# Two routed feed-forward layers and two image gates on one core: POOL's turn rewritten, column sums by halves, a square root moved ahead

## The chip, the cores and the metric

One core of one Trainium2 chip runs the whole program. The metric is device time in microseconds (us) of one launch. The kernel before took 1337.18 us, the median of 3 runs (1332.98 to 1341.03).

## The reference

`x` is (16, 256, 16, 16) in float32. All four steps add to their input:

```python
x = x + conv0(ln_c(x))     # 32 groups of 8 channels, gated by rows and columns
t = tokens(x);  t = t + ffn0(ln_t(t))   # 4096 tokens of 256, 8 experts, top 2
x = x + conv1(ln_c(x))     # 1x1 convolution 256 -> 256 with bias
t = tokens(x);  t = t + ffn1(ln_t(t))   # 8 experts, top 2, hidden 1024, biases

def branch(ph, pw):        # conv0, once with means, once with maxima
    hw = conv1x1(concatenate([ph, pw], axis=2))
    ah, aw = hw[:, :, :h], hw[:, :, h:]
    return gnorm(g * sigmoid(ah)[..., None] * sigmoid(aw)[:, :, None, :])
x1 = branch(g.mean(axis=3), g.mean(axis=2))
y1 = branch(g.max(axis=3), g.max(axis=2))
weights = softmax(mean of x1) . y1 + softmax(max of y1) . x1
out = g * sigmoid(weights)
```

In `ffn0` an expert is `silu(x w1) * (x w3)` times `w2` with hidden 512; in `ffn1` it is `silu(x v1 + b1)` times `v2` plus `b2` with hidden 1024.

## The kernel before, in words

Five engines run one instruction stream each and meet at semaphores: PE (matmul), DVE (vector), ACT (scalar), POOL (GpSimd) and SP (DMA queue). Nothing is scheduled by a planner; the order on each engine is the order of the source.

**First convolution.** The normed image is turned so that channels lie on partitions: `g`, two blocks `k` of 4096 values (16 images of 16 x 16). For `r` = 0 (sums) and 1 (maxima) and both `k`, DVE reduces every image along its rows (L1065) and along its columns (L1066, a strided view), 16 lines of 16 values each, and PE and ACT turn the lines into gates (L600, L838). POOL multiplies three of the four blocks `(r, k)` by the row gates (L239) and then by the column gates (L244), the third after DVE has given the gates of `r` = 1 their sign (L1088); DVE does the fourth with the same two operations. Both engines' inputs lie in SBUF. DVE then takes statistics (L1078), maxima (L1081), and the deviation (function `deviations(4)`: seven small operations, a square root by ACT at L805, five more from L1018). Softmax, a table of mixing weights and the last stage follow: for each of 16 images DVE writes four 128 x 128 masks (L1143, function `masks`), PE mixes (L617), ACT takes the sigmoid (L849), DVE multiplies, PE turns back, DVE adds and takes statistics.

**Pieces.** Beside this ACT sums absolute values of 64 pieces of 256 KB of the second layer's weights (`sum_pieces`, L830). SP loads them into three buffers, each as soon as the piece three before is summed. Pieces 0 to 19 stand in ACT's order ahead of the gates of `r` = 1, pieces 20 to 63 behind them and ahead of the square root.

**Expert stages.** Each layer sorts its 8192 token copies into 35 tiles of 256 rows, grouped by expert. For tile `n`: POOL gathers the rows by an indirect DMA each for two halves (`fetch`, L458) into one of two buffers `x_rows`; SP turns them by DMA transposes into one of two buffers `x_cols` (`turn_rows`, L360); PE multiplies up (L712) and down (L734); ACT and DVE work between; the result goes into the single buffer `y_rows`, and POOL adds it into DRAM by two indirect DMAs (`put`, L498). POOL's loop is by turns, one tile each: `put(n)` waits for tile n-1's stores to land, copies two lists of row numbers, waits for `y_copied` and issues the stores; then `fetch_next(n + 2)` copies two lists again (L505) and issues the gathers of tile n + 2. Each wait on a count that is a register stands in a loop of one pass (`after`).

In the first layer ACT does per tile: four silus (L927), four copies (L931), the high halves of one piece of the second layer's weights (`split_hi`, L903), then `move_pieces` (L911: two waits; L895: a store of 512 KB; L285, L286: two loads of 256 KB for the next tile's `split_hi`), and last the copy of the result into `y_rows` (L946). DVE multiplies (L1403), takes low halves (L1407), waits for `y_free`, chooses the next tile's token weights (`pick_weights`, L1380, L1383) and computes the low halves of the piece (L1337). In the second layer PE has 96 matmuls a tile, DVE writes the result (L1418), and ACT scales it (L953).

## Time and profile before

| | before |
|---|---|
| median of 3 runs | 1337.18 us |
| the profiled execution's own time | 1330.54 us |
| its span, first to last instruction | 1328.7 us |
| mean granted TensorE clock | 0.830 |
| busy, share of the span: PE, DVE, ACT, POOL | 72%, 61%, 45%, 38% |
| first convolution | from about 0 to 208 us |
| experts of layer 0, from the first copy of a result to the last | 382 to 721 us |
| second convolution and routing | about 730 to 895 us |
| experts of layer 1 | 905 to 1296 us |

Busy shares are averages over stages whose limits differ. What the change is worth is read stage by stage, from the wait that ends last there. In the rows below a start and a duration in us stand first; in brackets stands the idle time of the engine just before, and what ended it.

### The profile page before, as it was taken

What the parts mean: (1) busy time and instruction counts of PE and PEld (TensorE: products, weight loads), DVE (VectorE), ACT (ScalarE), POOL (GpSimd) and SP (SyncE); (2) the same over time, 40 slices, a digit from 0 to 9 for tenths busy, and PEclk for the clock granted to TensorE, in tenths of its full rate; (3) what the DMA queues carried; (4) which work ended last, traced back from release to release, by engine and by line L of the source; (5) the groups of instructions that cost most, each with busy time, mean ns of one, the idle gap of its engine ahead of it and who ended that gap; (6) DMA issues with size and microseconds to landing.
All of it is one profiled execution on the core that took longest, in us unless ns stands there. A gap on an engine that the chain in (4) does not pass through costs nothing.

```text
span 1328.7 us, 28374 instructions
## 1 busy us (share of the span) xinstructions
PE 954.9 (72%) x7185; PEld 790.8 (60%) x7185; DVE 806.6 (61%) x1970; ACT 595.0 (45%) x1332; POOL 509.3 (38%) x479
## 2 busy tenths in 40 slices
PE   5210375637688888888885388457999899999984
PEld 4100264624667666676774277426888787888873
DVE  6999488779755455455553676683455455555550
ACT  5265422228655555555553023283444344444442
POOL 1285000000036555666564140003555555556550
PEclk8655596555899999999998695558999999999996
DMA  7066204961857888888887704304555554554448
GB/s 254 1 198 209 75 0 118 337 186 48 269 125 183 182 180 174 186 194 192 192 182 182 257 0 153 109 1 95 120 104 117 127 122 85 135 134 75 77 74 264
DMA packets 210851, 189.97 MB, mean 143 GB/s; under 512 B 98992, under 2 KB 184440, under 8 KB 210680
## 3 DMA queue, kind: packets, MB, share of 16 engines
q1 hardware_dynamic: 150632, 108.48, 28.5%
q0 software_dynamic: 27440, 38.97, 18.3%
q10 hardware_dynamic: 32736, 42.02, 9.8%
q8 instruction: 18, 0.29, 0.1%
q14 instruction: 25, 0.20, 0.1%
HBM read 111.22 MB, written 58.79 MB: 128 GB/s over the span
## 4 chain that ended last, share of the span: by engine, by line
PE 34%; DMA 22%; issue 17%; DVE 11%; ACT 6%; ACTq 3%; POOL 2%; DVEq 1%; SPq 1%; POOLq 1%
PE bank L734 12%; PE bank L712 12%; DMA wreg<-in_L_ffn_w_dram 7%; DMA region<-rows_x,fetch_now 5%; DMA rows_y<-region,put_now 5%; PE bank L645 4%; DMA xt<-region 3%; PE bank L562 2%; PE bank L617 1%; POOL rows_y L498 1%; ACT wreg L830 1%; PE bank L770 1%; DVE region L1066 1%; PE bank L687 1%; DVE region L1418 1%
## 5 line engine op out<-in xcount | busy, mean ns | idle before, releaser
L712 PE MATMUL bank<-xt,wreg 128*128 x3360 | 391.0, 278 | 59.3 <-DMA xt<-region 52.1
L712 PEld LDWEIGHTS bank<-xt,wreg 128*128 128x128 f16 x3360 | 331.1, 100 | 113.5 <-issue 69.1
L498 POOL DMA_INDIRECT rows_y<-region,put_now x140 | 240.0, 1714 | 189.5 <-ACT region L953 87.7
L734 PE MATMUL bank<-wreg,region 128*128 128x256 f16 x2520 | 291.5, 274 | 24.0 <-DVE region L1413 13.9
L734 PEld LDWEIGHTS bank<-wreg,region 128*128 128x128 f16 x2520 | 242.4, 98 | 64.8 <-DVE region L1413 16.4
L458 POOL DMA_INDIRECT region<-rows_x,fetch_now x144 | 145.9, 1013 | 158.7 <-issue 82.6
L936 ACT ACTIVATE region<-bank,b_t,wreg 128x256 f32<-128x256 f32 x280 | 135.6, 562 | 20.6 <-issue 12.2
L953 ACT ACTIVATE region<-region 128x256 f32<-128x256 f32 x70 | 31.7, 500 | 207.3 <-DVE region L1418 202.0
L1410 DVE TENSOR_SCALAR region<-region,wreg 128x512 f16<-128x512 f32 x140 | 71.0, 507 | 65.6 <-ACT region L936 57.6
L1413 DVE SCALAR_TENSOR_TENSOR region<-region,wreg 128x512 f16<-128x512 f32 x140 | 105.2, 752 | 5.0
L562 PE MATMUL bank<-ident,xn 128*128 128x128 f32 x256 | 54.4, 372 | 58.9 <-DVE xn L1037 52.8
L1418 DVE SCALAR_TENSOR_TENSOR region<-bank,wreg,region 128x512 f32<-128x512 f32 x35 | 26.3, 751 | 109.8 <-PE bank L734 76.6
L1403 DVE SCALAR_TENSOR_TENSOR region<-bank,fac,region 128x256 f32<-128x256 f32 x140 | 64.1, 480 | 41.0 <-ACT region L927 33.6
L562 PEld LDWEIGHTS bank<-ident,xn 128*128 128x128 f32 x256 | 44.3, 202 | 66.8 <-DVE xn L1037 58.7
L927 ACT ACTIVATE region<-bank,fac 128x256 f32<-128x256 f32 x140 | 62.5, 470 | 37.2 <-PE bank L712 33.8
L645 PE MATMUL bank<-gate_w,xt 128*128 128x8 f32 x256 | 57.1, 361 | 18.8 <-DVE st_lg L1183 18.8
L645 PEld LDWEIGHTS bank<-gate_w,xt 128*128 128x128 f32 x256 | 55.8, 330 | 24.6 <-issue 24.1
L946 ACT ACTIVATE region<-bank,region 128x256 f32<-128x256 f32 x70 | 29.4, 471 | 86.1 <-issue 58.9
L1380 DVE TENSOR_TENSOR region<-region (+1 forms) x72 | 11.8, 163 | 92.5 <-DMA rows_y<-region,put_now 76.9
L1337 DVE SCALAR_TENSOR_TENSOR wreg<-wreg x70 | 49.5, 749 | 29.2 <-issue 24.6
L931 ACT ACTIVATE region<-region 128x256 f16<-128x256 f32 x140 | 57.1, 415 | 21.8 <-DVE region L1403 16.5
L458 POOL DMA_INDIRECT region<-rows_x,first_rows x4 | 4.4, 1099 | 155.0 <-DVE first_rows L1312 154.4
(241 smaller groups left out, 1312.5 us busy)
## 6 DMA issues: line engine op xcount, KB each, us to landing
wreg<-in_L_ffn_w_dram SPq DMA_DIRECT2D x48, 512.0 KB, 6.8
wreg<-in_L_ffn_w_dram ACTq DMA_DIRECT2D x72, 256.0 KB
split_v<-wreg ACTq DMA_DIRECT2D x36, 512.0 KB
wreg<-in_L_ffn_w_dram SPq DMA_DIRECT2D x64, 256.0 KB, 3.0
wreg<-split_v SPq DMA_DIRECT2D x32, 512.0 KB
rows_x<-region SPq DMA_DIRECT2D x16, 512.0 KB, 4.5
rows_y<-tok SPq DMA_DIRECT2D x16, 512.0 KB, 4.9
tok<-rows_y SPq DMA_DIRECT2D x16, 512.0 KB, 6.0
```

The lines of the kernel that those rows point to most:

```text
L458: nc.gpsimd.indirect_dma_start(x_bits[:, b, r, 0:C + 2], None, rows_x[f], bass.IndirectOffsetOnAxis(ap=row_list, axis=0)).then_inc(xr_load ...
L498: nc.gpsimd.indirect_dma_start(rows_y[f], bass.IndirectOffsetOnAxis(ap=put_now[:, g_:g_ + 1], axis=0), y_rows[:, g_, :], None, compute_op= ...
L562: last = pe.transpose(to[:, k, h * P:(h + 1) * P], xn[:, j, h, k * P:(k + 1) * P], ident[:])
L645: last = pe.matmul(zb[j][:, h * E:(h + 1) * E], xt[:, j, k, h * P:(h + 1) * P], gate_w[:, f, k], start=(k == 0), stop=(k == KC - 1))
L712: last = pe.matmul(to, block, x_cols[:, bass.ds(b, 1), :, xs_, k, :].rearrange("p j r n -> p (j r) n"), start=(k == 0 and ws_ + xs_ == 0), ...
L734: last = pe.matmul(yb[:, r * C:(r + 1) * C], lhs[:, c, r * P:(r + 1) * P], block, start=first, stop=end, skip_group_check=True)
L927: act.activation(gate_act[:, h, (c % 2) * TILE:(c % 2 + 1) * TILE], zb[c][:, 0:TILE], ACT.Silu, scale=fac[f][:, 0, e:e + 1]).then_inc(silu ...
L931: act.activation(hid_hi[:, c], hid[:, h, (c % 2) * TILE:(c % 2 + 1) * TILE], ACT.Copy).then_inc(hi_ready[f], 1)
L936: last = act.activation(gate_act[:, h, c * TILE:(c + 1) * TILE], zb[h][:, c * TILE:(c + 1) * TILE], ACT.Silu, bias=b1_t[:, e, 2 * h + c:2 ...
L1403: dve.scalar_tensor_tensor(half(hid[:, h], c), zb[c][:, TILE:2 * TILE], fac[f][:, 1, e:e + 1], half(gate_act[:, h], c), ALU.mult, ALU.mult ...
L1410: dve.tensor_scalar(to_hi, gate_act[:, h], fac[f][:, 1, e:e + 1], None, ALU.mult).then_inc(hi_ready[f], 1)
L1413: dve.scalar_tensor_tensor(to_lo, gate_act[:, h], fac[f][:, 1, e:e + 1], to_hi, ALU.mult, ALU.subtract).then_inc(lo_ready[f], 1)
```

## The change

1. **POOL's turn.** Three tiles are gathered ahead of the loop instead of two having been fetched and a third begun. A turn `t` copies all four lists at once into one of two buffers (`copy_lists`), gathers tile t + 3, and then stores tile t. The gathers wait for the transposes of tile t + 1 and for its token weights. DVE therefore picks the weights of tile n + 1 at the top of tile n's body, into four slots rather than two. In layer 0 DVE no longer waits for `y_free`.
2. **ACT in layer 0.** `move_pieces` stands behind the copy of the result.
3. **Column lines.** The strided reduction becomes four tensor_tensor operations: the 16 x 16 image is added (or compared) by halves, 2048, 1024, 512 and 256 values wide.
4. **Square root ahead of sums.** ACT takes the square root after 46 pieces, four more follow, and the other 14 stand by twos behind the sigmoids of the mixing loop, which is unrolled on ACT.
5. **Masks.** Four operations become one tensor_tensor with two broadcast inputs.

```diff
-                for r in range(2):
-                    fetch(f, 0, r, first_rows[:, r:r + 1])
+                def first_fetch(n):
+                    for r in range(2):
+                        free(pool, xr_loaded[r][f], 16 * n)
+                        free(pool, xc_ready[r][f], 16 * (n - 1))
+                        free(pool, weights_ready[f], n - 1)
+                        fetch(f, n % 2, r, first_rows[:, 2 * n + r:2 * n + r + 1])
+                first_fetch(0)
                 total = pool.value_load(bounds[0:1, E:E + 1], min_val=E, max_val=TILES)
+                first_fetch(1)
...
-                def put(n, copied):
-                    pool.wait_ge(y_free[f], 32 * n + 16)
-                    nc.gpsimd.tensor_copy(put_now[:], moves[:, bass.ds(2 * n, 2), 1]).then_inc(puts_copied[f], 1)
-                    after(n, lambda m: pool.wait_ge(puts_copied[f], m + 1))
-                    after(copied, lambda m: pool.wait_ge(y_copied[f], m))
...
                 with pool.Fori(0, total // 2) as p:
                     for b in range(2):
-                        put(2 * p + b, 2 * p + b + 1)
-                        fetch_next(2 * p + b + 2, 1 - b)
+                        t = 2 * p + b
+                        for r in range(2):
+                            pool.wait_ge(xr_loaded[r][f], 16 * t + 48)
+                        copy_lists(t, b)
+                        def may_fetch(m):
+                            pool.wait_ge(lists_copied[f], m + 1)
+                            for r in range(2):
+                                pool.wait_ge(xc_ready[r][f], 16 * m + 32)
+                            pool.wait_ge(weights_ready[f], m + 2)
+                        after(t, may_fetch)
+                        for r in range(2):
+                            fetch(f, 1 - b, r, now[:, b, r, 0:1])
+                        after(t, lambda m: pool.wait_ge(y_copied[f], m + 1))
+                        put(b)
...
-            sum_pieces(20, 2 * PIECES)
+            sum_pieces(20, 46)
             deviation(4)
+            sum_pieces(46, 50)
...
-            pairs(act, mix_gates)
+            for i in range(HB):
+                mix_gates(i)
+                sum_pieces(50 + 2 * i, min(52 + 2 * i, 2 * PIECES))
...
                             split_hi(n)
-                            move_pieces(n)
                             act.wait_ge(y_ready[f], n + 1)
...
                             last.then_inc(y_copied[f], 1)
+                            move_pieces(n)
...
-                    dve.tensor_reduce(line[:, r, k, :, HW:2 * HW], v.rearrange("p b h w -> p b w h"), AX.X, op).then_inc(lines_ready, 1)
+                    half, n = g[:, k, :].rearrange("p (b n) -> p b n", b=NB), L // 2
+                    free(dve, lines_ready, 2 * (r * KC + k))
+                    while n > HW:
+                        chain(dve.tensor_tensor(fold[:, :, 0:n], half[:, :, 0:n], half[:, :, n:2 * n], op))
+                        half, n = fold, n // 2
+                    dve.tensor_tensor(line[:, r, k, :, HW:2 * HW], half[:, :, 0:HW], half[:, :, HW:2 * HW], op).then_inc(lines_ready, 1)
...
-                for r in range(2):
-                    for k in range(KC):
-                        last = dve.tensor_scalar(mix[:, j, r, k], in_group[:], coef[:, r, k, bass.ds(2 * i + j, 1)],
-                                                 None, ALU.mult)
-                last.then_inc(mix_ready[j], 1)
+                dve.tensor_tensor(mix[:, j].rearrange("p r k n -> p (r k) n"), in_group[:].unsqueeze(1).to_broadcast([P, 2 * KC, P]),
+                                  coef[:, :, :, bass.ds(2 * i + j, 1)].rearrange("p r k b -> p (r k) b").to_broadcast([P, 2 * KC, P]),
+                                  ALU.mult).then_inc(mix_ready[j], 1)
...
                     with dve.Fori(edges[e], edges[e + 1]) as n:
+                        pick_weights(f, n + 1)
...
-                        else:
-                            dve.wait_ge(y_free[f], 32 * n + 16)
-                        pick_weights(f, n + 1)
```

DVE's stream in the first convolution, before, from the first lines to the signs (`wreg` is `g`, `region` holds the lines and the partial sums):

```order
L1057 TENSOR_TENSOR region<-region 128x128
L1065 TENSOR_REDUCE region<-wreg 128x16x16
L1066 TENSOR_REDUCE region<-wreg 128x16x16
L1065 TENSOR_REDUCE region<-wreg 128x16x16
L1066 TENSOR_REDUCE region<-wreg 128x16x16
```

The same two blocks after the change:

```order
L1076 TENSOR_TENSOR region<-region 128x128
L1084 TENSOR_REDUCE region<-wreg 128x16x16
L1088 TENSOR_TENSOR region<-wreg 128x2048
L1088 TENSOR_TENSOR region<-region 128x16x64
L1088 TENSOR_TENSOR region<-region 128x16x32
L1090 TENSOR_TENSOR region<-region 128x16x16
L1084 TENSOR_REDUCE region<-wreg 128x16x16
L1088 TENSOR_TENSOR region<-wreg 128x2048
L1088 TENSOR_TENSOR region<-region 128x16x64
L1088 TENSOR_TENSOR region<-region 128x16x32
L1090 TENSOR_TENSOR region<-region 128x16x16
```

Each column reduction, one operation with one input, became four operations with two inputs in SBUF. They stand in the stretch in which POOL's gates run.

ACT's stream in one tile of layer 0, before, from the second high half of the piece (L903) to the store of the last piece (L895), ahead of which stand the two waits of `move_pieces` (L911); the two loads and then the copy of the result follow:

```order
L903 ACTIVATE wreg<-wreg 128x512
L911 UNCONDITIONAL_BRANCH
L911 ISA x2
L911 COMPARE_AND_BRANCH
L911 UNCONDITIONAL_BRANCH
L911 ISA
L911 COMPARE_AND_BRANCH
L895 ISA x3
L895 DMA split_v<-wreg 128x2048
```

And after, from the same high half (L922) on; L964 is the copy of the result, and L930 begins the waits of `move_pieces`, behind which the store and the loads stand:

```order
L922 ACTIVATE wreg<-wreg 128x512
L960 REGISTER_ALU
L961 ISA
L964 ISA
L964 ACTIVATE region<-bank,region 128x256
L964 ISA
L964 ACTIVATE region<-bank,region 128x256
L930 UNCONDITIONAL_BRANCH
L930 ISA
```

The two ACTIVATEs of the result, and the waits they carry, now stand between the high halves of a piece and the loads of the next piece.

## Rows read from the trace of the kernel before

**Rows 1.** Timeline, first convolution, DVE and POOL: start, us, engine, line.

```profile
45.34 6.97 DVE L1066 TENSOR_REDUCE region<-wreg 128x256 f32<-128x4096 f32 x1
52.23 4.41 DVE L1065 TENSOR_REDUCE region<-wreg 128x256 f32<-128x4096 f32 x1
...
56.75 7.18 POOL L239 TENSOR_TENSOR wreg<-wreg,region 128x4096 f32<-128x4096 f32 x1 [52.24 <-ACT region L838]
...
64.01 8.87 POOL L244 TENSOR_TENSOR wreg<-wreg,region 128x4096 f32<-128x4096 f32 x1
...
80.10 8.88 POOL L244 TENSOR_TENSOR wreg<-wreg,region 128x4096 f32<-128x4096 f32 x1
...
86.56 2.43 DVE L1072 TENSOR_TENSOR region<-region 128x1 f32<-128x1 f32 x1
...
94.90 4.43 DVE L239 TENSOR_TENSOR wreg<-wreg,region 128x4096 f32<-128x4096 f32 x1
94.94 11.41 POOL L239 TENSOR_TENSOR wreg<-wreg,region 128x4096 f32<-128x4096 f32 x1 [5.97 <-DVE region L1088]
...
99.36 11.28 DVE L244 TENSOR_TENSOR wreg<-wreg,region 128x4096 f32<-128x4096 f32 x1
```

**Rows 2.** Timeline, pieces 20 and 63 on ACT, and DVE behind the square root.

```profile
91.59 0.62 ACT L830 ACTIVATE wreg<-wreg 128x512 f32<-128x512 f32 x1
...
145.06 0.63 ACT L830 ACTIVATE wreg<-wreg 128x512 f32<-128x512 f32 x1 [0.71 <-DMA wreg<-in_L_ffn_w_dram]
...
147.38 0.55 DVE L1018 RECIPROCAL xt<-xt 128x64 f32<-128x64 f32 x1 [10.52 <-ACT xt L805]
```

**Rows 3.** Timeline, mixing loop, DVE: a product of 512 values, then four masks.

```profile
161.83 0.69 DVE L1153 TENSOR_TENSOR region<-region,wreg 128x512 f32<-128x512 f32 x1 [4.09 <-ACT region L849]
162.44 0.87 DVE L1143 TENSOR_SCALAR region<-region 128x128 f32<-128x128 f32 x4
```

**Rows 4.** Timeline, experts of layer 0, ACT: the first and the last copy of a result.

```profile
382.11 0.84 ACT L946 ACTIVATE region<-bank,region 128x256 f32<-128x256 f32 x2 [2.38 <-DVE region L1393]
...
721.29 0.84 ACT L946 ACTIVATE region<-bank,region 128x256 f32<-128x256 f32 x2 [3.68 <-issue]
```

**Rows 5.** Timeline, experts of layer 0, ACT and its queue: from loads to next result.

```profile
410.45 0.40 ACTq L286 DMA_DIRECT2D wreg<-in_L_ffn_w_dram  x1
...
411.15 0.84 ACT L946 ACTIVATE region<-bank,region 128x256 f32<-128x256 f32 x2 [2.27 <-issue]
...
416.54 1.33 ACT L903 ACTIVATE wreg<-wreg  x2 [1.04 <-DMA wreg<-in_L_ffn_w_dram]
...
420.14 0.84 ACT L946 ACTIVATE region<-bank,region 128x256 f32<-128x256 f32 x2 [2.26 <-issue]
```

**Rows 6.** Timeline, experts of layer 0: one turn of POOL, and the landing of stores.

```profile
595.27 1.62 POOL L498 DMA_INDIRECT rows_y<-region,put_now  x1 [2.31 <-ACT region L946]
...
597.20 1.58 POOL L498 DMA_INDIRECT rows_y<-region,put_now  x1 [0.30 <-issue]
...
600.46 1.04 POOL L458 DMA_INDIRECT region<-rows_x,fetch_now  x1 [1.48 <-DMA xt<-region]
...
602.42 0.16 DVE L1380 TENSOR_TENSOR region<-region  x1 [3.52 <-DMA rows_y<-region,put_now]
602.56 0.84 ACT L946 ACTIVATE region<-bank,region 128x256 f32<-128x256 f32 x2 [2.35 <-DMA rows_y<-region,put_now]
...
604.33 1.62 POOL L498 DMA_INDIRECT rows_y<-region,put_now  x1 [1.35 <-ACT region L946]
```

**Rows 7.** Timeline, experts of layer 0, PE: the up part of three tiles.

```profile
400.29 5.43 PE L712 MATMUL bank<-xt,wreg 128*128 x48 [1.65 <-DMA xt<-region]
408.40 5.43 PE L712 MATMUL bank<-xt,wreg 128*128 x48
419.57 7.10 PE L712 MATMUL bank<-xt,wreg 128*128 x48 [2.90 <-DMA xt<-region]
```

**Rows 8.** Waits over the whole span: DVE's result of layer 1 behind stores.

```profile
DVE region L1418 <- DMA rows_y<-region,put_now: 33.2, 6, 7.2
```

More of the change, by code:

```diff
@@ L83, in bass_metaformer @@
         sig = region[:, 2048:4096].rearrange("p (r k b l) -> p r k b l", r=2, k=KC, b=NB)
+        fold = region[:, 4096:6144].rearrange("p (b n) -> p b n", b=NB)
         rows = region[:, :].bitcast(F16).rearrange("p (t c) -> p t c", t=NT)
@@ L259, in bass_metaformer @@
         listed, list_taken = sem("listed"), sem("list_taken")
-        fetches_copied, puts_copied = two("fetches_copied"), two("puts_copied")
+        lists_copied = two("lists_copied")
         ids_listed = sem("ids_listed")
@@ L526, in all_done, with may_put @@
+                        put(b)
+                last = total // 2 * 2
+                copy_lists(last, 0)
+                def may_put(m):
+                    pool.wait_ge(lists_copied[f], m + 1)
+                    pool.wait_ge(y_free[f], 32 * m + 16)
+                after(last, may_put)
+                after(total, lambda m: pool.wait_ge(y_copied[f], m))
+                put(0)
                 def all_done(m):
@@ L1377, in pick_weights @@
                     dve.wait_ge(xr_loaded[r][f], 16 * n + 16)
-                side = n if isinstance(n, int) else n % 2
-                one = lambda v: v[:, bass.ds(side, 1)]
-                dve.tensor_tensor(one(weighed), one(x_weights), choice[:, bass.ds(2 * n, 2), :].rearrange("p (j g) k -> p j g k", j=1),
+                one = lambda v, sides: v[:, bass.ds(n if isinstance(n, int) else n % sides, 1)]
+                dve.tensor_tensor(one(weighed, 2), one(x_weights, 2), choice[:, bass.ds(2 * n, 2), :].rearrange("p (j g) k -> p j g k", j=1),
                                   ALU.mult).then_inc(weighed_ready[f], 1)
                 dve.wait_ge(weighed_ready[f], n + 1)
-                dve.tensor_reduce(one(weights), one(weighed), AX.X, ALU.add).then_inc(weights_ready[f], 1)
+                dve.tensor_reduce(one(weights, 4), one(weighed, 2), AX.X, ALU.add).then_inc(weights_ready[f], 1)
             def experts(f, edges):
```

40 lines of the change are left out of this document (14 added, 26 removed).

## The prediction

> **What bounds the kernel now.** I read the busy time by stretches first, to see the stages, then the timeline of the three places that the diff touches, and the waits last. No engine is full over the whole span; each stage has its own limit.
>
> In the first convolution DVE is busy nearly without a gap, and POOL's gates run beside it. The thing to see there is how the two engines treat each other [rows 1]. POOL's row gates take 7.18 us alone and its column gates 8.87. The third time, started 0.04 us after DVE's own L239, the row gates take 11.41: 7.18 plus 4.23, which is DVE's whole operation. DVE's L244, issued at 99.36, takes 11.28 though it has the size of L239 (4.43): 6.85 more, about what POOL still had to do (94.94 + 11.41 = 106.35). And L1072, a product of one element per partition, takes 2.43 us: it ends at 88.99, when POOL's L244 ends (80.10 + 8.88 = 88.98). So a tensor_tensor on DVE with both inputs in SBUF and a running POOL gate exclude each other for a whole instruction, and at an end the one that has waited goes first. The reductions L1065 and L1066 (4.41 and 6.97 us) are not slowed beside POOL: with one input they pass.
>
> Behind that, DVE is ready for the square root at 147.38 - 10.52 = 136.86 and waits 10.52 us, since ACT first finishes all 64 pieces [rows 2].
>
> In the experts of layer 0 a tile takes (721.29 - 382.11) / 34 = 9.98 us [rows 4]. PE alone needs 8.11: where it had no wait, up part followed up part at that distance [rows 7]. PE waits for the transposes, hence for the gathers, which POOL issues behind the stores. POOL's turn has hardly a pause of its own choice: 595.27 to 604.33 is stores, copy, gathers, copy [rows 6]. Two other loops run close behind. The store loop: stores at 595.27, landed by 602.4, copy of the result at 602.56, next stores at 604.33, which makes 9.06 us [rows 6]. The loop of the pieces: loads issued by 410.85, landed by 416.54 (5.7 us; the idle time before L903 is laid to this DMA), then high halves, waits, a store, two loads and the result at 420.14 [rows 5]; this gives 420.14 - 411.15 = 8.99 us.
>
> In the experts of layer 1 PE is nearly full; stores held DVE up six times, for 33.2 us of DVE's time, of which PE lost only part [rows 8].
>
> **The change part by part.**
>
> Column lines. By 4.43 us for 4096 values and 0.69 for 512 [rows 1, 3] a value costs 1.04 ns and an operation 0.15 us. The four steps (2048, 1024, 512, 256 values) cost 2.29 + 1.22 + 0.69 + 0.42, and with the gaps between 4.75, against 6.97: 2.2 less per block, if they are let through. Now the order of events, by the rule read from rows 1:
> - Block (0,0) ends at 45.3 + 4.8 = 50.1. The next row reduction ends at 54.5. POOL's first gate followed these lines by 56.75 - 52.31 = 4.4, so it too wants to start at 54.5. Whoever is first, one half-sum (2.3), POOL's 7.2, POOL's 8.9 (which gets its turn at the first gap in DVE's chain) and the other half-sums (2.4) come one after another: the lines of (0,1) are ready at 75.3, not at 63.6.
> - POOL's second gates start some 3 us later (the 4.4 without the loading of ACT's table), at 78.4. DVE reduces rows until 79.7 and then waits until 85.6; a half-sum to 87.9, POOL to 96.8, the rest to 99.2.
> - Block (1,1) has no POOL beside it, which waits for the signs: 4.4 + 4.8, to 108.4. Before, the lines were done at 86.3. That is 22.1 later; L1072 no longer waits 2.3, so the signs and all behind them are 19.9 later (94.9 becomes 114.8), and DVE is ready for the square root at 156.8.
>
> The Trainium skill has this as a rule that speaks against the change: in "SBUF — State Buffer", section "Who interferes with whom", a DVE instruction with two SBUF inputs and a GpSimd instruction that reads SBUF hold the shared port in turn, each for its whole length, while a tensor_reduce on trn2 never contends. By that rule the stage ends 10 us later, without it 17 us earlier; the trace agrees with it, by the 2.43 us of L1072.
>
> Square root ahead. A piece takes (145.06 - 91.59) / 43 = 1.24 us [rows 2]. Pieces 20 to 45 begin behind the gates of r = 1, now at about 111.4, and end at 144, before 156.8. So the wait of 10.5 us is gone: L1018 comes at about 157.2 in place of 147.38, which is 9.8 later. The four pieces behind the root (three are loaded, the fourth's load can be issued only after the first) and the load of the table for the exponential push it back by 0 to 1 us more, I take 0.7. The 14 others fit into ACT's idle time in the mixing loop, where ACT works less than half of it; if they did not, each pair would cost up to 1.5 us for 7 rounds.
>
> Masks. One product of 512 values (0.69) for four masks (0.87) [rows 3]. In the loop DVE already waits for PE, so only the first mask's distance to PE counts: about 0.1 us for 8 rounds, 0.8; between 0 and 3. **The convolution stage: 9.8 + 0.7 - 0.8, about 10 us longer** (8 to 12).
>
> POOL's turn in layer 0. The copy ahead of the stores goes, with its 1.35 to 1.5 us of waiting for the list; the gathers stand a tile earlier, so neither PE nor SP waits for them: tile t + 3 is asked for about two tiles before its transposes are due. POOL's turn falls from 9 to about 7.7 us and no longer binds. Late next is what ACT does. The result now stands ahead of the loads: between high halves and loads come the preparation of the copy, 0.3 us (410.85 to 411.15), and at most its two ACTIVATEs, 0.84 [rows 5]. The loop of the pieces becomes 9.0 + 0.3 at the least (the queue runs ahead of the engine), 9.0 + 1.14 at the most. No row shows how far the queue runs ahead of ACT; I take 0.55 and so 9.55 us, above PE's 8.11 and the store loop's 9.06. That gives 34 x (9.98 - 9.55) = 14.6 us. At the end of the stage the last result was held for 3.68 us by `move_pieces` [rows 4]; it goes, 3.7. **Layer 0: 18.3 us shorter** (from 1.7 longer, at 10.14, to 35 shorter, at 9.06). A side effect is in this: PE at half clock (7.10 in place of 5.43, after 2.90 of idle [rows 7]) comes up five times in the stage, and shorter idle stretches should make it rarer.
>
> DVE's earlier choice of the weights costs nothing: the tile it needs has landed by then, and the work is the same 0.3 us. The dropped wait for `y_free` was beside ACT's own wait for the same stores.
>
> Layer 1. The gathers were hidden there already, the store loop (single `y_rows`) is as long as before, since the stores follow `y_copied` by the same path, and PE sets the pace. The bias is loaded some 3 us later, behind the second gather; DVE used it about 5 us after it had landed. I take 0, between -3 and +3.
>
> Sum: +10 - 18.3 + 0 = -8.3 us. The profiled execution took 1330.5 us, so it would be 1322; the median of the runs lies 6.6 above it, and on that the forecast is 1337.2 - 8.3 = **1329 us**.
>
> **The rivals.**
> - *Slower: the loads become the bound.* Place: ACT in layer 0, between L903 and L285. If ACT's queue cannot run ahead, the whole copy enters the loop: 10.14 us a tile, a loss of 5.4 that the end's 3.7 only partly repays. With the convolution's 10 the kernel takes 1337.2 + 1.7 + 10 = 1349. It decides from 0.8 us of added time on (9.8 us a tile pays for the convolution exactly). For it: five splits already wait for their load. Against it: the gathers and transposes move out of the window in which the loads run, so 5.7 may shrink.
> - *The loads give way.* Without gathers and transposes beside them they land early, and the store loop rules: 9.06 a tile, 35 shorter, less 10: 1312.
> - *The half-sums are let through* (contiguous halves might behave differently from the strided gates). Lines end 8.8 earlier, the signs about 7 earlier (pieces 0 to 19 still stand before the gates), and the 10.5 wait goes as well: 17 shorter, with layer 0 in all 35: 1302. Against it stand three rows.
>
> **How the numbers follow.** A measurement of this kernel can tell about 0.5%, 6.7 us, from no change, so faster means below 1330.5. Forecast case 0.62, its own range 1320 to 1338 (9.3 to 9.8 us a tile); slightly more than half of it, 0.35, lies below 1330.5. Loads bound: 0.16, slower. Loads give way: 0.12. Half-sums let through: 0.10. Faster 0.35 + 0.12 + 0.10 = 0.57, the same 0.27, slower 0.16. The range 1308 to 1347 leaves out most of the last case and half of the first rival.
>
> **What would show it.** In the profile after: a half-sum of 2048 values that takes 7 to 10 us and one of 1024 that takes over 8, in blocks (0,1) and (1,0), against 2.3 and 1.2 in the other two; the reciprocal of the deviation at about 157 without a wait for ACT; in layer 0 results 9.5 us apart with ACT's L922 waiting for its load, and no wait of PE for the transposes; layer 1 as before. The forecast is wrong if all half-sums are short, if results come 10 us apart, or if another wait (the stores') stands in ACT's copy.

## The result, and the profile after

The kernel after takes 1303.84 us (median of 4 runs, 1295.59 to 1306.07), the kernel before in the same comparison 1339.11 (1332.98 to 1342.13): ratio 0.9731, 95% interval 0.9674 to 0.9788. It is 35 us faster than before, and the time lies 4 us below the lower end of the forecast range. The profiled execution of after took 1302.36 us with a span of 1300.5; that is 28.2 under the profiled execution of before, whose own 1330.54 lies 8.6 under the median of its runs. The sum below is made between the two traces.

| from the traces, us | before | after | moved by | forecast |
|---|---|---|---|---|
| first maximum of the first routing (behind the convolution) | 213.98 | 220.97 | +7.0 | +10 |
| first result of layer 0 | 382.11 | 392.10 | +3.0 more | 0 |
| layer 0, first to last result | 339.2 | 312.0 | -27.2 | -18.3 |
| last result of layer 0 to first of layer 1 | 196.5 | 197.8 | +1.3 | 0 |
| layer 1, first to last result | 373.5 | 360.8 | -12.7 | 0 |

Timeline of after, first convolution, DVE and POOL (start, us, engine, line); it answers to [rows 1, 2]:

```profile
54.32 2.28 DVE L1088 TENSOR_TENSOR region<-wreg 128x2048 f32<-128x2048 f32 x1
54.51 9.12 POOL L241 TENSOR_TENSOR wreg<-wreg,region 128x4096 f32<-128x4096 f32 x1 [50.02 <-ACT region L854]
56.63 17.29 DVE L1088 TENSOR_TENSOR region<-region 128x1024 f32<-128x1024 f32 x2
...
63.71 9.66 POOL L246 TENSOR_TENSOR wreg<-wreg,region 128x4096 f32<-128x4096 f32 x1
...
77.31 7.17 POOL L241 TENSOR_TENSOR wreg<-wreg,region 128x4096 f32<-128x4096 f32 x1 [3.94 <-ACT region L854]
78.63 8.00 DVE L1088 TENSOR_TENSOR region<-wreg 128x2048 f32<-128x2048 f32 x1
84.56 10.75 POOL L246 TENSOR_TENSOR wreg<-wreg,region 128x4096 f32<-128x4096 f32 x1
86.66 10.46 DVE L1088 TENSOR_TENSOR region<-region 128x1024 f32<-128x1024 f32 x2
...
112.27 0.60 DVE L1112 TENSOR_SCALAR region<-region 128x256 f32<-128x256 f32 x2
...
155.19 0.55 DVE L1037 RECIPROCAL xt<-xt 128x64 f32<-128x64 f32 x1 [0.32 <-ACT xt L821]
```

The engines take turns, instruction by instruction. POOL's first gate starts 0.19 us behind a half-sum and takes 9.12, its own 7.18 and 1.94 more; the half-sum still had 2.09. The two half-sums behind it take 17.29 where they need 1.95. The half-sum at 78.63 ends at 86.63, 2.1 us after POOL's row gate ended at 84.48: it ran then, and POOL's column gate, which wanted to start at 84.56, ran behind it. The deviation's reciprocal waits 0.32 us for the square root, no longer 10.52.

Waits of PE and ACT in the experts of layer 0, before (382 to 721.3 us; columns: waited for, us in total, times, longest):

```profile
PE bank L712 <- DMA xt<-region: 37.8, 21, 3.1
PE bank L734 <- ACT region L931: 7.0, 17, 1.1
...
ACT wreg L903 <- DMA wreg<-in_L_ffn_w_dram: 4.1, 5, 1.0
```

The same after (392 to 704.1 us):

```profile
PE bank L750 <- ACT region L950: 18.1, 45, 2.0
...
ACT wreg L922 <- DMA wreg<-in_L_ffn_w_dram: 2.2, 2, 1.3
```

PE's wait for the transposes is gone whole, 37.8 us, and 11 us come back as a wait of its down part for ACT. PE is busy for 287.5 of the 312.0 us, before for 284.2 of 339.2. ACT waits for its load twice in 35 tiles. The mean tile is 312.0 / 34 = 9.18 us. Results came at a distance of 10.0 to 11.1 us in the first five tiles and of 8.98 on average behind them. The side effect that the prediction named came too: before, the granted clock fell from 1.0 to 0.5 (2.4 to 1.2 GHz) for 3.4 us five times in this stage, each time after a wait of 2.3 to 2.9 us for the transposes, and the up part took 7.0 to 7.1 us in place of 5.43 [rows 7]. After, it fell once, at 398.7 us, in a down part behind 2.0 us of idle time. This alone does not shorten the layer: in moves_only, below, the clock fell once too, and its layer 0 is longer than before.

One tile of after, timeline, answering to [rows 5 to 7]:

```profile
522.08 1.03 POOL L460 DMA_INDIRECT region<-rows_x,region  x1 [1.26 <-issue]
522.78 1.33 ACT L922 ACTIVATE wreg<-wreg  x2 [0.36 <-issue]
...
523.67 5.44 PE L728 MATMUL bank<-xt,wreg 128*128 x48
524.48 0.84 ACT L964 ACTIVATE region<-bank,region 128x256 f32<-128x256 f32 x2 [0.36 <-PE bank L750]
...
527.20 0.40 ACTq L288 DMA_DIRECT2D wreg<-in_L_ffn_w_dram  x1
527.96 0.84 ACT L946 ACTIVATE region<-bank,fac 128x256 f32<-128x256 f32 x2 [2.64 <-PE bank L728]
...
529.45 1.51 PE L750 MATMUL bank<-wreg,region 128*128 128x256 f16 x12 [0.34 <-ACT region L950]
...
531.86 1.33 ACT L922 ACTIVATE wreg<-wreg  x2 [0.35 <-issue]
532.75 5.44 PE L728 MATMUL bank<-xt,wreg 128*128 x48
```

PE's up part follows at 532.75, 9.08 us later, with 0.6 us of pauses in between: PE sets the pace. From L922 to the end of the loads' issue (527.60) it takes 4.82 us, and the loads land within 4.26, since L922 does not wait for them at 531.86.

Layer 1, a change of expert. Timeline of before, POOL, SP's queue and DVE:

```profile
952.01 2.61 SPq L360 DMA_TRANSPOSE xt<-region  x2
...
954.68 1.79 POOL L498 DMA_INDIRECT rows_y<-region,put_now  x1 [3.27 <-ACT region L953]
955.20 1.74 SPq L365 DMA_DIRECT2D wreg<-split_v  x4
956.78 1.84 POOL L498 DMA_INDIRECT rows_y<-region,put_now  x1 [0.31 <-issue]
...
964.99 0.75 DVE L1418 SCALAR_TENSOR_TENSOR region<-bank,wreg,region 128x512 f32<-128x512 f32 x1 [5.36 <-DMA rows_y<-region,put_now]
```

And of after:

```profile
929.68 2.61 SPq L362 DMA_TRANSPOSE xt<-region  x2
...
935.32 1.82 SPq L367 DMA_DIRECT2D wreg<-split_v  x4
938.01 1.78 POOL L509 DMA_INDIRECT rows_y<-region  x1 [3.31 <-ACT region L972]
940.10 1.86 POOL L509 DMA_INDIRECT rows_y<-region  x1 [0.30 <-issue]
...
946.31 0.75 DVE L1440 SCALAR_TENSOR_TENSOR region<-bank,wreg,region 128x512 f32<-128x512 f32 x1 [3.35 <-PE bank L750]
```

SP issues the four loads of the weights (`load_v`) behind the transposes of the tile after next (`turn_rows`) and behind the result of the expert's last tile. Before, those transposes waited for gathers that POOL had issued behind the stores of the tile before; at all six changes of expert the loads followed them by 0.6 us and went out 0.5 to 3.4 us behind the first store. Here they went out between the two stores, which then landed 10 us after the first was issued. After, the transposes are long done, the loads follow the result, 2.7 us ahead of the first store, and here the result waits for PE alone. At the six changes of expert DVE's idle time ahead of the result is 3.8 us on average after (3.06 to 4.45) and 5.5 before (3.96 to 7.15); about 2.7 of that is the usual wait for PE.

### The profile page after: what moved, and what is told of

It is laid out like the page before. It is cut to its first block, busy times and chain, and to the rows that moved or that the text cites. A ratio compares the mean times of both kernels' runs of the same rounds, so it can differ in the third digit from the quotient of the medians.

```text
span 1300.5 us, 26761 instructions
## 1 busy us (share of the span) xinstructions
PE 956.0 (74%) x7185; PEld 780.9 (60%) x7185; DVE 826.7 (64%) x1934; ACT 591.3 (45%) x1332; POOL 510.3 (39%) x407
## 3 DMA queue, kind: packets, MB, share of 16 engines
q0 software_dynamic: 27440, 38.97, 17.7%
## 4 chain that ended last, share of the span: by engine, by line
PE 35%; DVE 18%; issue 16%; DMA 14%; ACT 8%; ACTq 6%; DVEq 1%; POOL 1%; SPq 1%; POOLq 0%
PE bank L750 13%; PE bank L728 11%; DMA wreg<-in_L_ffn_w_dram 4%; PE bank L661 4%; DMA rows_y<-region 4%; DVE region L1088 4%; PE bank L578 2%; DMA region<-rows_x,region 2%; DVE xt L1102 2%; ACTq L287 2%; ACT region L946 2%; ACT region L950 1%; ACTq L914 1%; PE bank L633 1%; DVE region L1084 1%
## 5 line engine op out<-in xcount | busy, mean ns | idle before, releaser
L728 PE MATMUL bank<-xt,wreg 128*128 x3360 | 383.5, 274 | 18.8 <-DMA xt<-region 13.0
L728 PEld LDWEIGHTS bank<-xt,wreg 128*128 128x128 f16 x3360 | 327.2, 98 | 69.4 <-issue 28.6
L509 POOL DMA_INDIRECT rows_y<-region x140 | 247.6, 1769 | 185.1 <-ACT region L972 93.6
L750 PE MATMUL bank<-wreg,region 128*128 128x256 f16 x2520 | 296.1, 274 | 24.9 <-ACT region L950 18.1
L750 PEld LDWEIGHTS bank<-wreg,region 128*128 128x128 f16 x2520 | 235.6, 98 | 80.6 <-ACT region L950 31.0
L460 POOL DMA_INDIRECT region<-rows_x,region x148 | 149.6, 1011 | 309.8 <-DVE region L1334 154.4
L946 ACT ACTIVATE region<-bank,fac 128x256 f32<-128x256 f32 x140 | 58.3, 465 | 92.5 <-PE bank L728 55.9
L686 PE MATMUL bank<-xt,xn 128*128 128x160 f16 x128 | 38.4, 314 | 35.0 <-ACT xt L902 34.3
L504 POOL COPY region<-routed 128x4 uint32 x70 | 62.3, 890 | 4.1 <-DMA region<-rows_x,region 4.1
L1429 DVE TENSOR_TENSOR region<-region 128x256 f16<-128x256 f32 x140 | 57.4, 427 | 6.4 <-ACT region L950 0.3
```

What stands on the lines that cost most here:

```text
L460: nc.gpsimd.indirect_dma_start(x_bits[:, b, r, 0:C + 2], None, rows_x[f], bass.IndirectOffsetOnAxis(ap=row_list, axis=0)).then_inc(xr_load ...
L504: nc.gpsimd.tensor_copy(now[:, b], moves[:, bass.ds(2 * t, 2), :]).then_inc(lists_copied[f], 1)
L509: nc.gpsimd.indirect_dma_start(rows_y[f], bass.IndirectOffsetOnAxis(ap=now[:, b, g_, 1:2], axis=0), y_rows[:, g_, :], None, compute_op=ALU ...
L728: last = pe.matmul(to, block, x_cols[:, bass.ds(b, 1), :, xs_, k, :].rearrange("p j r n -> p (j r) n"), start=(k == 0 and ws_ + xs_ == 0), ...
L750: last = pe.matmul(yb[:, r * C:(r + 1) * C], lhs[:, c, r * P:(r + 1) * P], block, start=first, stop=end, skip_group_check=True)
L946: act.activation(gate_act[:, h, (c % 2) * TILE:(c % 2 + 1) * TILE], zb[c][:, 0:TILE], ACT.Silu, scale=fac[f][:, 0, e:e + 1]).then_inc(silu ...
```

## Experiments

Every kernel was run beside the kernel before; ratios are to it. The median of before moved from 1332.4 to 1341.2 us between the groups of runs, so kernels of different groups are compared by ratio. The first four kernels form one group, moves_undone, no_folds, stores_first and three_parts the second, and after_again, loads_late, gates_held and best the third. Stages are read from one trace each. "Signs" is the start of the sign operation on DVE (94.27 us in before), "reciprocal" that of the deviation (147.38).

### The parts alone

**folds_only**, the kernel before with part 3 of the change alone (shortened):

```diff
-    dve.tensor_reduce(line[:, r, k, :, HW:2 * HW], v.rearrange("p b h w -> p b w h"), AX.X, op)
+    while n > HW:
+        chain(dve.tensor_tensor(fold[:, :, 0:n], half[:, :, 0:n], half[:, :, n:2 * n], op))
```

> The kernel before with the column lines by halves alone. Theory (half-sums and POOL's gates exclude each other): signs about 18 us later than before, as in the kernel after (112.3 against 94.9), and since the square root still stands behind all 64 pieces, which now start behind gates that come 18 us later, the root follows at about 147.4 + 18 = 165; the whole kernel 17 to 20 us slower, ratio 1.013 to 1.015. Rival (the folds cost only what the finished kernel's convolution lost, since the root's wait would absorb a part): 7 to 9 us slower, ratio 1.005 to 1.007.

Measured: 1358.09 against 1335.32 us, ratio 1.0151 (1.0098 to 1.0204); signs at 112.5, reciprocal at 164.35, still behind a wait of 9.23 us for the root. So the folds alone cost 17 us in the convolution, and in the kernel after only the square root moved ahead keeps this from its end. The medians differ by 22.8 us, where 17 to 20 were expected; in the trace layer 0 is another 5.0 us longer, 344.2 in place of 339.2, with ten up parts of PE over 7 us where before has six.

**sqrt_only**, part 4 alone:

```diff
-            sum_pieces(20, 2 * PIECES)
+            sum_pieces(20, 46)
             deviation(4)
+            sum_pieces(46, 50)
```

> The kernel before with the square root ahead of the last 18 pieces alone. Theory: the 10.52 us wait of DVE goes, 9.5 to 10.5 us faster, ratio 0.992 to 0.993; the reciprocal of the deviation at 137 to 138. Rival (the root's gain needs the later lines, since pieces 20 to 45 are not summed by 137): a wait of several us stays and the gain is under 6 us. Both expect experts as before (9.98 us a tile in layer 0, 10.98 in layer 1).

Measured: 1329.84 us, ratio 0.9943 (0.9906 to 0.9980); reciprocal at 137.35, the first routing 9.35 us earlier in the trace. The theory holds for the convolution, but of the 9.5 to 10.5 us only 5.5 arrive at the end: in the trace the stretch from there to layer 0 took 173.7 us in place of 168.1. The 14 pieces in the mixing loop cost nothing there: DVE's rounds are 6.03 us apart as before. In kernels that also have the masks in one operation they are 5.84.

**pool_only**, part 1 alone, with the pieces moved ahead of the result as before:

```diff
+                        for r in range(2):
+                            fetch(f, 1 - b, r, now[:, b, r, 0:1])
+                        after(t, lambda m: pool.wait_ge(y_copied[f], m + 1))
+                        put(b)
```

> The kernel before with POOL's new turn and DVE's earlier choice of the weights alone; ACT still moves the pieces ahead of the result. Theory (the gathers ahead of the stores remove PE's wait for the transposes, and the pieces' loop never bound but in a few tiles): layer 0 from its first to its last result 312 to 317 us in place of 339.2 (9.2 to 9.3 a tile), layer 1 360.8 in place of 373.5, kernel 34 to 40 us faster, ratio 0.970 to 0.975. Rival (the move of the pieces behind the result is what shortens layer 0, by letting the stores start 2.5 us earlier): layer 0 above 325 us, kernel 15 to 25 us faster.

Measured: 1286.91 us, ratio 0.9624 (0.9570 to 0.9679). Layer 0 takes 303.0 us (8.91 a tile, better than the 9.2 expected), layer 1 360.9. It is 48.4 us faster than before: this part alone gains more than the whole change.

**moves_only**, part 2 alone:

```diff
                             split_hi(n)
-                            move_pieces(n)
...
                             last.then_inc(y_copied[f], 1)
+                            move_pieces(n)
```

> The kernel before with the pieces' store and loads behind the copy of the result, in layer 0, alone. Theory (POOL's gathers behind its stores still hold the transposes): 3.7 us at the end of the stage and up to 0.2 us a tile, 4 to 11 us faster, ratio 0.992 to 0.997. Rival (the earlier stores are what layer 0 gained): layer 0 at about 9.3 us a tile, 20 to 27 us faster, ratio 0.980 to 0.985. Forecast on record (the loads bound the pieces' loop at 9.55 us a tile or more): slower tiles where ACT's high halves wait for their load, no more than 5 us of gain, possibly a loss.

Measured: 1340.63 us, ratio 1.0029 (0.9993 to 1.0065), layer 0 at 344.2 us in place of 339.2. My theory and its first rival both missed: there is no gain, as the forecast on record allowed. What happened is the loop that I had forecast for the kernel after. ACT's waits in layer 0 of this kernel (before: 4.1 us in 5 tiles), and one tile of its timeline:

```profile
ACT wreg L903 <- DMA wreg<-in_L_ffn_w_dram: 31.3, 22, 3.1
```

```profile
504.45 1.33 ACT L903 ACTIVATE wreg<-wreg  x2 [0.43 <-issue]
...
508.65 0.68 ACTq L286 DMA_DIRECT2D wreg<-in_L_ffn_w_dram  x1
514.41 1.33 ACT L903 ACTIVATE wreg<-wreg  x2 [1.06 <-DMA wreg<-in_L_ffn_w_dram]
```

From the high halves to the end of the loads' issue 4.88 us, then 5.08 until they land: 9.96 for this tile.

### The parts taken back

**moves_undone**, the kernel after with part 2 taken back:

```diff
                             split_hi(n)
+                            move_pieces(n)
...
-                            move_pieces(n)
```

> The kernel after with the pieces' store and loads ahead of the result again. Theory from the runs so far (behind the result they stand ahead of the next tile's first silu on ACT, and PE's down part waits for it): layer 0 from first to last result 303 us (8.9 a tile) in place of 312, ACT's silu about 3 us earlier in a tile, PE's wait for the high halves of the hidden values under 9 us in place of 18; kernel about 9 us faster than after, 1294 to 1297, ratio to before 0.966. Rival (the 9 us between the two kernels are the few slow tiles at the start of the stage, from other causes): layer 0 at 309 to 312, kernel as after, 0.973.

Measured: 1293.18 us, ratio 0.9709 (0.9679 to 0.9739); layer 0 305.1 us. The trace is 7 us shorter there, but the ratio is that of the kernel after (0.9731, and 0.9697 when it was run again), so the medians don't show the 7 us. PE's wait for ACT was 16.5 us (385 to 700 us), against 17.7 in after, and not under 9: the explanation by ACT's silu that stands in the expectation is not borne out.

**no_folds**, the kernel after with part 3 taken back, the strided reductions again:

```diff
+                    dve.tensor_reduce(line[:, r, k, :, HW:2 * HW], v.rearrange("p b h w -> p b w h"), AX.X, op).then_inc(lines_ready, 1)
```

> The kernel after with the strided reductions again. Theory (half-sums and POOL's gates exclude each other): signs at 94 in place of 112.3, the reciprocal of the deviation at 137.5 in place of 155.2, kernel 17 to 18 us faster than after, about 1286, ratio to before 0.960. Rival (beside earlier lines the 46 pieces or POOL hold the root): the reciprocal above 145, gain under 10.

Measured: 1272.52 us, ratio 0.9551 (0.9519 to 0.9584); signs at 93.8, reciprocal at 136.69, the first routing 18.2 us earlier than in after. The folds are a loss of 18 us in the convolution. By the ratios the whole kernel is 20 to 24 us faster than after, not 17 to 18: layer 0 took 303.9 us here, 8 less than in after, which the theory did not say.

**stores_first**, the kernel after with its gathers behind its stores:

```diff
-                        after(t, may_fetch)
-                        for r in range(2):
-                            fetch(f, 1 - b, r, now[:, b, r, 0:1])
+                        after(t, lambda m: pool.wait_ge(lists_copied[f], m + 1))
                         after(t, lambda m: pool.wait_ge(y_copied[f], m + 1))
                         put(b)
+                        after(t, may_fetch)
+                        for r in range(2):
+                            fetch(f, 1 - b, r, now[:, b, r, 0:1])
```

> The kernel after with POOL's stores of tile t ahead of the gathers of tile t + 3, in both layers; four lists in one copy and three tiles ahead kept. Theory (the order of gathers and stores is what counts): PE waits again for the transposes in layer 0, which goes back to 330 us or more (9.7 a tile), and in layer 1 the loads of the next expert's weights go out later than 2 us after the tile's start and meet the stores, 370 us or more; kernel 25 us or more slower than after. Rival (gathering three tiles ahead is enough, since a gather then has a tile more until it is needed): layer 0 within 4 us of 312 and layer 1 within 3 us of 361, kernel as after.

Measured: 1335.22 us, ratio 1.0032 (1.0008 to 1.0057); layer 0 339.2 us, layer 1 367.7 (theory 370 or more). So beside the moved pieces the third tile ahead and the lists copied at once bring layer 0 nothing without the new order, and in layer 1 5.8 of the 12.7 us. What they would bring with the pieces ahead of the result, as in pool_only, was not run. And the wait is another than expected. Waits of stores_first, of PE from 385 to 700 us, of ACT and POOL from 450 to 690:

```profile
PE bank L729 <- DMA xt<-region: 3.2, 9, 0.6
```

```profile
ACT wreg L923 <- DMA wreg<-in_L_ffn_w_dram: 35.7, 25, 1.9
```

```profile
POOL region L504 <- DMA region<-rows_x,region: 50.8, 24, 2.9
```

PE hardly waits for transposes, so the third tile ahead took that wait away, and the loads took its place: ACT waits for them in 31 of 35 tiles, and POOL waits for the gathers that it has just issued, since one copy of four lists now wants them landed. Timeline of ACT there:

```profile
599.47 1.33 ACT L923 ACTIVATE wreg<-wreg  x2 [1.19 <-DMA wreg<-in_L_ffn_w_dram]
...
603.65 0.85 ACTq L288 DMA_DIRECT2D wreg<-in_L_ffn_w_dram  x1
609.98 1.33 ACT L923 ACTIVATE wreg<-wreg  x2 [1.49 <-DMA wreg<-in_L_ffn_w_dram]
```

Loads that are issued by 604.50 land at 609.98, 5.48 us later. I took the same distance, from the end of the loads' issue to the next high halves, for every tile of the traces. Where ACT waited it is the landing as ACT sees it; where it did not, it is an upper bound.

| | ACT waited: tiles, mean (least) | did not: tiles, least |
|---|---|---|
| before | 5, 5.69 (5.24) | 30, 5.07 |
| pool_only | 10, 5.42 (5.18) | 25, 4.93 |
| moves_only | 22, 5.40 (4.54) | 13, 4.26 |
| stores_first | 31, 5.37 (4.81) | 4, 5.53 |
| moves_undone | 12, 5.63 (5.19) | 23, 4.92 |
| after | 2, 5.11 (4.88) | 33, 4.22 |
| after_again | 7, 4.75 (4.45) | 28, 4.23 |
| no_folds | 9, 4.76 (4.56) | 25, 4.24 |

With gathers ahead and pieces behind, as in after, the loads land about 0.7 us sooner than in any other order. It takes both: in stores_first, where only POOL's order differs, they don't, nor in pool_only, where only the pieces' does. The waits are the slow cases, but the semaphores' own updates, which some traces hold nearly whole, agree for all tiles: from the end of the issue to the last update it takes 3.75 us on average in no_folds, and 4.63 in stores_first, 4.41 in moves_undone, 4.40 in three_parts. ACT starts 0.62 us or more behind that update, which the distances above include.

**after_again**, the kernel after unchanged, since layer 0 at 312.0 stood against 303 to 305 us in four relatives:

> The kernel after, unchanged, a second time: how much of the 312.0 us of its layer 0 belongs to that one execution. If the tiles of 10 to 11 us at the start of the stage come from its order (pieces moved behind the result), 309 to 314 us again and a ratio near 0.973. If they belong to one execution, 303 to 307 us, as in the kernel without folds, whose experts' code is the same, and a ratio under 0.972.

Measured: 1300.62 us, ratio 0.9697 (0.9668 to 0.9725); layer 0 313.1 us, with the same five slow tiles, though the ratio is below the 0.972 that was to speak for one execution. In the traces it belongs to the kernel. With POOL's new order layer 0 takes 312.0 to 315.7 us in the four traces that have both folds and moved pieces (after, this one, and the first two below), 305.1 with folds alone, 303.9 with moved pieces alone, 303.0 and 304.3 with neither (pool_only, three_parts). No code of that stage differs between the first group and no_folds. About half of the 8 us lies in the first five tiles. Why the two together cost 8 us stays open.

### Layer 1 and the lock

"The lock" is short for what the first profile shows: a two-input operation of DVE on SBUF and a gate of POOL exclude each other for a whole instruction.

**loads_late**, the kernel after with SP's loads of the next expert's weights held until ACT has scaled the result:

```diff
                         with sp.Fori(edges[e + 1], edges[e + 1] + 1) as m:
-                            sp.wait_ge(y_ready[1], m)
+                            sp.wait_ge(y_copied[1], m)
```

> The kernel after; in layer 1 SP issues the loads of the next expert's second weights only when ACT has scaled the result of the expert's last tile (about 2 us later than in after, just before POOL stores that result). Theory (layer 1 gained since these loads now go out ahead of the stores, not between them): the result of the next tile waits 4 to 7 us for the stores at each of the six changes of expert, PE's wait for the low halves rises from 3 to 10 us or more, layer 1 368 to 373 us in place of 360.8, kernel 7 to 12 us slower than after. Rival (layer 1 gained by the shorter turn of POOL, or the stores landed earlier for another reason): layer 1 within 3 us of 361.

Measured: 1310.90 us, ratio 0.9764 (0.9734 to 0.9793), beside 1300.62 and 0.9697 for after_again: 9 to 10 us slower. Layer 1 takes 372.8 us, before it was 373.5. Timeline, and the waits from 900 to 1275 us:

```profile
936.55 1.81 SPq L367 DMA_DIRECT2D wreg<-split_v  x4
937.26 1.79 POOL L509 DMA_INDIRECT rows_y<-region  x1 [3.30 <-ACT region L972]
...
947.01 0.75 DVE L1440 SCALAR_TENSOR_TENSOR region<-bank,wreg,region 128x512 f32<-128x512 f32 x1 [4.79 <-DMA rows_y<-region]
```

```profile
DVE region L1440 <- DMA rows_y<-region: 46.5, 12, 6.4
...
PE bank L750 <- DVE region L1435: 11.6, 9, 2.6
```

PE's wait is 3.2 us in after and 13.9 in before. The loads go out 0.7 us ahead of the first store in place of 2.7. The transposes behind them on SP's queue are not held: at this change they start 5.53 us behind the start of the last result, as in after, and at none of the six more than 0.3 us later. So the edit moves nothing but these loads, and it brings back 12.0 of the 12.7 us. That is where layer 1 gained.

**gates_held**, the kernel after with POOL's gates behind all lines:

```diff
+            pool.wait_ge(lines_ready, 8)
             for n, (r, k) in enumerate(((0, 0), (0, 1), (1, 1))):
```

> The kernel after, with POOL's first gate held until all eight sets of lines are done. Theory (half-sums and POOL's gates exclude each other, nothing else slows the half-sums): all four half-sums of 2048 values take 2.28 us and the eight of 1024 and 512 together under 8 us, the lines are done at 77 to 78, signs at 98 to 100 in place of 112.3, and though POOL starts 23 us later the reciprocal of the deviation comes at 144 to 147 in place of 155.2; kernel 8 to 11 us faster than after. Rival (the long half-sums have another cause, memory or the order of waits): some half-sum stays above 5 us, and the kernel is slower by the time POOL lost.

Measured: 1298.89 us, ratio 0.9674 (0.9644 to 0.9704), equal to after_again within the intervals, where 8 to 11 us less were expected. All sixteen half-sums are short, and the signs come at 98.53; the reciprocal comes at 151.66, where 144 to 147 was expected. Timeline of DVE and POOL:

```profile
72.08 2.28 DVE L1089 TENSOR_TENSOR region<-wreg 128x2048 f32<-128x2048 f32 x1
74.40 1.95 DVE L1089 TENSOR_TENSOR region<-region 128x1024 f32<-128x1024 f32 x2
...
77.07 7.18 POOL L241 TENSOR_TENSOR wreg<-wreg,region 128x4096 f32<-128x4096 f32 x1 [72.58 <-DVE region L1091]
77.09 7.17 DVE L1097 TENSOR_TENSOR region<-region 128x1 f32<-128x1 f32 x1
...
98.53 10.81 DVE L1113 TENSOR_SCALAR region<-region 128x256 f32<-128x256 f32 x2
100.37 8.83 POOL L246 TENSOR_TENSOR wreg<-wreg,region 128x4096 f32<-128x4096 f32 x1
```

A product of one element per partition, issued 0.02 us behind POOL's gate, takes the gate's own 7.17. And the sign operations, with one tensor input, take 10.81 us beside POOL's gates in place of 0.60: they are held too. These 10.2 us are what the expectation lacked: without them, by my estimate, the reciprocal would have come at about 141.5.

**best**, POOL's turn, square root ahead and masks, without folds and moves, but with three edits by the rule of the lock; the same kernel without these edits is **three_parts**:

> The kernel before with POOL's turn, the square root ahead and the masks in one operation; no folds, pieces moved ahead of the result. If the parts add, pool_only's 48 us, the root's 8 to 9 and the masks' 1.3 give 57 to 60 us less than before: 1276 to 1279, ratio 0.955 to 0.958. Rival (earlier stages give back what the weights' loads or the clock then take): above 1283.

Measured: 1272.93 us against 1332.40, ratio 0.9553 (0.9521 to 0.9585); layer 0 304.3, layer 1 358.7. It is 59.5 us less than before, so the parts add. It equals no_folds (1272.52), so once the gathers have their new place, moving the pieces is worth nothing that can be measured. The three edits of best, shortened:

```diff
+                    if r == 0 and k == 0:
+                        while n > HW:
+                            chain(dve.tensor_tensor(fold[:, :, 0:n], half[:, :, 0:n], half[:, :, n:2 * n], op))
...
-            chain(dve.tensor_tensor(size, sign, gn_w_, ALU.mult))
+            chain(dve.tensor_scalar(size, sign, gn_w_, None, ALU.mult))
...
             gate_by_rows(dve, 1, 0).then_inc(gated_mid, 1)
+            dve.wait_ge(gated_by_pool, 2)
+            channel_stats(0, 1)
             dve.wait_ge(gated_mid, 1)
             gate_by_columns(dve, 1, 0).then_inc(gated_mid, 1)
-            dve.wait_ge(gated_by_pool, 2)
-            channel_stats(0, 1)
```

> POOL's turn, square root ahead and masks in one operation as in three_parts, and three edits by the rule of the folds: halves for block (0,0) alone, where POOL is idle; the one-element product of the signs as a tensor_scalar, which has one tensor input; the statistics of block (0,1) between DVE's row gates and column gates of block (1,0), beside POOL's row gates. Theory: the half-sums short (4.75 us), the product 0.15 us in place of 2.4, signs at 90; DVE's column gates take 5 to 7 us in place of 11.3, with the statistics unslowed beside POOL; the reciprocal at 127 to 129 in place of 137.1; kernel 8 to 10 us faster than three_parts, 1263 to 1266, ratio to before 0.947 to 0.949. Rival (POOL's third block comes late instead): the reciprocal above 133.

Measured: 1265.84 us, ratio 0.9445 (0.9415 to 0.9475), the fastest kernel here. Timeline of DVE:

```profile
44.67 2.28 DVE L1088 TENSOR_TENSOR region<-wreg 128x2048 f32<-128x2048 f32 x1
...
83.65 0.21 DVE L1098 TENSOR_SCALAR region<-region 128x1 f32<-128x1 f32 x1
...
94.11 5.32 DVE L1104 BATCH_NORM_STATS2 xt<-wreg 128x6 f32<-128x256 f32 x16
99.35 6.17 DVE L246 TENSOR_TENSOR wreg<-wreg,region 128x4096 f32<-128x4096 f32 x1
...
126.96 0.55 DVE L1037 RECIPROCAL xt<-xt 128x64 f32<-128x64 f32 x1 [0.32 <-ACT xt L821]
```

The statistics are not slowed beside POOL, the column gates behind them wait 1.7 us instead of 6.9, and the reciprocal comes 10.1 us earlier than in three_parts. The span is only 5.4 shorter, since the experts took 3.8 us more in this execution and the stretch between them 1.7. Against three_parts the median is 7.1 us less, and 14 by the ratios; 8 to 10 were expected.

## Why the prediction was wrong

The direction was right, the size was not: 8 us forecast, 28 between the traces and 35 between the medians.

**Column lines: right.** The order of events by turns gave the lines of (0,1) at 75.3, of (1,0) at 99.2 and of (1,1) at 108.4, DVE's first gate behind the signs at 114.8 (94.90 before; the signs themselves went from 94.27 to 112.27) and the reciprocal at 157.2. The trace has 74.4, 97.6, 106.5, 112.9 and 155.2. folds_only (+17), no_folds (-18) and gates_held (all half-sums short once POOL waits) show that it is POOL's gates that lengthen them. The Trainium skill's "SBUF — State Buffer", section "Who interferes with whom", has it that a DVE instruction with two SBUF inputs contends with a GpSimd instruction that reads SBUF; the trace agrees, by the 17.29 us of two half-sums that need 1.95.

**Square root and masks: right.** The wait is gone (sqrt_only, reciprocal at 137.35), and the masks gave 0.19 us a round, about 1.3 in all, where 0.8 was forecast. The stage came out at +7.0, below my 8 to 12, mostly since the lines came 2 us earlier than worked out.

**"Nine and a half us a tile, bound by the pieces' loop": this step failed.** The added time was not 0.55 but 1.5 us, above even my upper bound: from the high halves to the end of the loads' issue 4.82 in place of 3.3. What saved the tile is the other term of the loop, 5.7 us, which the sum kept as it was; that it may shrink stood only among the rivals. I had taken the 5.7 us in which loads landed from tiles in which ACT waited for them, five of 35 in before: the slow ones, and of the old order. In after 33 of 35 tiles did not wait, and one of them bounds the landing by 4.22. With the gathers put behind the stores again it is 5.4, and the tile 9.98 (stores_first); in the old order the moved pieces make single tiles of 9.96 (moves_only). So the mechanism of my forecast is real in two kernels, and absent in the one that I forecast. The rival "the loads give way" had the loads right and came with 0.12; its 9.06 us a tile, from the store loop, is near the measured 9.18 by luck, since PE sets that pace and not the stores. That layer 0 still takes 8 us more than in the kernels without folds or without moved pieces has no cause that was shown. The 3.7 us at the end went as forecast: the last copy follows the high halves without a wait.

**"Layer 1: I take 0": this step failed, and by more.** It gained 12.7 us, with bounds of 3. I had named the waits [rows 8] and kept them, because the store loop keeps its length. I had not followed SP's queue: `load_v` stands behind the transposes, and earlier gathers move it from behind a tile's first store to 2.7 us ahead of it. loads_late gives 12.0 us of it back by this move alone. A step that is moved had to be followed on every queue that waits for it, and here I followed POOL's only.

The 3.0 us between the convolution and the first result of layer 0 are not part of the change: among the kernels of this study that stretch takes 168 to 176 us without a relation to their edits that I can see, and before's execution had the shortest, 168.1.

## What to carry to other kernels

A duration read from waits is a sample of the slow cases and belongs to the transfers that lay beside them: look also at how short a time sufficed in a tile that did not wait, and give the term a range to both sides. When a step moves, list what stands behind it on each queue and in front of which other transfer it will now go out. On DVE, place operations that pass beside POOL (reductions, statistics) between those that don't, and take the parts of a change apart: here one part gave more than the whole gain and another took 18 us of it in the convolution.

## What was not expected of the hardware

- A tensor_scalar of 256 fp32 values with one tensor input is held by POOL's gates like a tensor_tensor: 10.81 us for two in gates_held, 0.60 without POOL. One of a single value took 0.21 beside POOL (best), where the tensor_tensor of a single value took 7.17. The Trainium skill's "SBUF — State Buffer", section "Who interferes with whom", names the first: a tensor_scalar can enter a mode that uses both of DVE's ports, and then contends with GpSimd. The trace agrees for 256 values; which condition spares the single value no run here shows.
- Two loads of 256 KB landed on average 5.4 to 5.7 us after their issue, where ACT waited for them, in five kernels with other orders of the transfers beside them, and 4.8 to 5.1 us in the order of after, after_again and no_folds, where the least bound is 4.2, though the bytes are the same. Which of the transfers makes the difference was not separated.
- Four weight loads issued 0.5 to 3.4 us behind the first store of a tile (before) or 0.7 us ahead of it (loads_late) left DVE idle ahead of the next result for 5.5 and 5.4 us on average over the six changes of expert, and 2.7 us ahead of it (after) for 3.8.
